# A state-space stage in which VectorE takes over one of two weighting products from POOL

## The reference, cut to what matters

```python
def step(h, inp):
    u_t, dt_t, B_t, C_t = inp
    dA = jnp.exp(-dt_t[..., None] * A)
    h = dA * h + (dt_t * u_t)[..., None] * B_t[:, None, :]
    y = jnp.einsum('bdn,bn->bd', h, C_t)
    return (h, y)
```

## Time and profile before

| what | us |
|---|---|
| median of three runs | 7111.84 |
| lowest and highest of them | 7104.78, 7119.30 |
| the profiled execution | 7122.96 |
| its span, first to last instruction | 7121.2 |

### The profile page before, as it was taken

One profiled execution on the slowest core, in us unless ns is written; L12 is line 12 of the kernel. 1 busy time (PEld: TensorE's weight loads), 2 busy tenths in 40 slices (PEclk: granted clock), 3 DMA queues, 4 the chain that ended last, 5 costly groups with the idle time before them and its releaser, 6 DMA issues. The chain is left out here.

```text
span 7121.2 us, 150074 instructions
## 1 busy us (share of the span) xinstructions
PE 5984.3 (84%) x47596; PEld 3842.3 (54%) x47596; DVE 5970.1 (84%) x12264; ACT 3439.2 (48%) x6820; POOL 2652.3 (37%) x1391
## 2 busy tenths in 40 slices
PE   5777888888888887988988988986888888888888
PEld 1224555555555554565565566565555555555555
DVE  5988888888888885998998998996979797979796
ACT  3335666666666662222222222222657575656565
POOL 1444444444444441122122122221535353535353
PEclk7998999999999998998998998988999999999999
DMA  0002222222222210000000000000212121212121
GB/s 14 0 0 63 59 52 59 52 59 52 59 52 59 53 46 13 1 1 1 1 1 1 1 1 1 1 0 16 60 50 61 51 60 51 63 49 62 50 63 37
DMA packets 159623, 244.44 MB, mean 34 GB/s; under 512 B 36596, under 2 KB 57008, under 8 KB 157494
## 3 DMA queue, kind: packets, MB, share of 16 engines
q1 hardware_dynamic: 159158, 238.71, 13.3%
HBM read 36.20 MB, written 1.05 MB: 5 GB/s over the span
## 5 line engine op out<-in xcount | busy, mean ns | idle before, releaser
L879 POOL TENSOR_TENSOR f_rope<-f_rope,f_t 128x1024 f32<-128x1024 f32 x384 | 918.5, 2392 | 1247.7 <-DVE f_t L775 1247.7
L1315 PE MATMUL psum<-tk_kT,tk_qs 128*128 128x512 f32 (+3 forms) x4128 | 1263.7, 467 | 9.1 <-POOL tk_qs L1548 9.1
L882 POOL TENSOR_TENSOR f_rope<-f_rope,f_rn 128x1024 f32<-128x1024 f32 x384 | 903.7, 2353 | 778.3 <-DVE f_rn L762 763.3
L1548 POOL TENSOR_TENSOR tk_qs<-tk_qT,tk_mix 128x1024 f32<-128x1024 f32 x258 | 499.2, 1938 | 1587.5 <-PE psum L1316 1423.2
L1315 PEld LDWEIGHTS psum<-tk_kT,tk_qs 128*128 128x128 f32 x4128 | 757.3, 208 | 440.5 <-issue 298.4
L775 DVE TENSOR_TENSOR f_t<-f_raw,f_rot 128x512 f32<-128x512 f32 x768 | 903.0, 1214 | 0.0
L454 PE MATMUL psum<-f_wqkv,f_xs 128*128 128x512 f32 x1536 | 785.0, 619 | 104.2 <-DMA f_wqkv<-in_Wqkv 56.1
L1505 DVE MAX8 tk_m<-tk_work 128x8 f32<-128x528 f32 (+3 forms) x1792 | 818.4, 497 | 2.0 <-DVE tk_work L1511 1.5
L1511 DVE MATCH_REPLACE8 tk_work<-tk_m,tk_work 128x400 f32<-128x400 f32 (+3 forms) x1536 | 745.3, 492 | 1.3 <-issue 1.0
L771 DVE TENSOR_TENSOR f_rope<-f_raw,f_rot 128x1024 f32<-128x1024 f32 x384 | 582.9, 1518 | 20.7 <-ACT f_raw L600 19.6
L600 ACT ACTIVATE f_raw<-psum 128x512 f32<-128x512 f32 x768 | 454.6, 595 | 249.2 <-PE psum L454 209.4
(11 more groups left out here) (234 smaller groups left out, 10764.0 us busy)
## 6 DMA issues: line engine op xcount, KB each, us to landing
f_v<-f_v_tok SPq DMA_DIRECT2D x1152, 128.0 KB, 2.4
f_v<-f_v_tok SPq DMA_DIRECT2D x768, 64.0 KB, 2.0
f_wqkv<-in_Wqkv SPq DMA_DIRECT2D x12, 1536.0 KB, 6.7
f_wo<-in_Wo SPq DMA_DIRECT2D x12, 512.0 KB, 4.1
f_w<-in_W SPq DMA_DIRECT2D x12, 341.0 KB
f_w<-in_W SPq DMA_DIRECT2D x24, 64.0 KB
tk_wkv<-in_Wkv SPq DMA_DIRECT2D x1, 1024.0 KB, 6.0
out<-y_tok SPq DMA_DIRECT2D x4, 256.0 KB, 2.5
```

Source lines behind the costliest of these rows:

```text
L879: pool.tensor_tensor(part, part, t2[:, half, :, :], ALU.add).then_inc(s["rope_added"], 1)
L882: pool.tensor_tensor(part, part, rn[:, H * half:H * (half + 1)].unsqueeze(2).to_broadcast([P, H, DH]), ALU.mult).then_inc(s["add_done"], 1)
L1315: pe.matmul(psum[:, j, 0:n], qs[:, j, c, :], kT[:, c, 0:n], start=(c == 0), stop=False, skip_group_check=True)
L1548: pool.tensor_tensor(qs[:, j, :, :], qT[:, :, P * t:P * (t + 1)], mix[:, :, heads(p, j)].to_broadcast([P, PAIRS, P]), ALU.mult).then_inc(s ...
```

## The change

In the state-space block POOL forms `hc` for channel 0 alone. For channel 1 VectorE forms it, reading C from its PSUM bank and not from the copy `c_sb`. VectorE's product of index n - 1 stands in its program between `dbu` and the scan of channel 1 of index n; the last one, of index 15, follows the last scan. The semaphore `hc_done` becomes two, `hc0_done` and `hc1_done`. TensorE waits in addition for `hc1_done` of n - 2 before it spreads B and C of n, since C's bank has VectorE as a reader too. ACT's copy of C now waits for channel 0's product of n - 2 alone, and channel 1's scan has no wait of its own for `hc` any more. The whole diff:

```diff
--- before.py
+++ after.py
@@ -895,7 +895,7 @@
     with ExitStack() as ctx:
         load = names(ctx, "mw", nc, "loaded", "turned", "copied", "done")
         s = names(ctx, "mb", nc, "zeroed", "xz_full", "xz_evac", "conv_in", "conv_step", "silu", "u_done", "xd_full", "xd_evac", "dt_full", "dt_in", "dt_abs",
-                  "dt_exp", "dt_ln", "dt_max", "dt_done", "sel", "bc_full", "b_used", "c_copied", "da_done", "dbu", "scanned", "hc_done",
+                  "dt_exp", "dt_ln", "dt_max", "dt_done", "sel", "bc_full", "b_used", "c_copied", "da_done", "dbu", "scanned", "hc0_done", "hc1_done",
                   "y_full", "y_evac", "y_step", "yg_done", "out_full", "out_done", "staged", "copied", "scrap")
 
         def sb(name, shape, dt=F32):
@@ -1064,7 +1064,7 @@
                 with pe.Fori(0, B) as b:
                     def sums(n):
                         for c in range(CI):
-                            pe.wait_ge(s["hc_done"], 1 + CI * DS * b + CI * n + c + 1)
+                            pe.wait_ge(s[f"hc{c}_done"], 1 + DS * b + n + 1)
                             if n == 0 and c == 0:
                                 pe.wait_ge(s["y_evac"], 1 + CI * b)
                             pe.matmul(psum[:, 4 + c, :], k.ident[:, :], hc[:, (CI * n + c) % 4, :], start=(n == 0), stop=(n == DS - 1),
@@ -1074,9 +1074,11 @@
                         if n >= 2:
                             pe.wait_ge(s["b_used"], 1 + CI * (DS * b + n - 1))
                             pe.wait_ge(s["c_copied"], 1 + DS * b + n - 1)
+                            pe.wait_ge(s["hc1_done"], 1 + DS * b + n - 1)
                         else:
                             pe.wait_ge(s["b_used"], 1 + CI * DS * b)
                             pe.wait_ge(s["c_copied"], 1 + DS * b)
+                            pe.wait_ge(s["hc1_done"], 1 + DS * b)
                         for which in range(2):
                             pe.matmul(psum[:, 2 * which + n % 2, :], sel[:, DS * which + n, :], batch3(xd, b, P), start=True, stop=True).then_inc(s["bc_full"], 1)
                         if n >= 2:
@@ -1099,9 +1101,9 @@
                             act.activation(da[:, (CI * n + c) % 4, :], batch(dt, c, b), ACT.Exp, scale=neg_a[:, c, n:n + 1]).then_inc(s["da_done"], 1)
                         act.wait_ge(s["bc_full"], 1 + 2 * (DS * b + n) + 2)
                         if n >= 2:
-                            act.wait_ge(s["hc_done"], 1 + m0 - 2)
+                            act.wait_ge(s["hc0_done"], 1 + DS * b + n - 1)
                         else:
-                            act.wait_ge(s["hc_done"], 1 + CI * DS * b)
+                            act.wait_ge(s["hc0_done"], 1 + DS * b)
                         act.activation(c_sb[:, n % 2, :], psum[:, 2 + n % 2, :], ACT.Copy).then_inc(s["c_copied"], 1)
 
             @block.vector
@@ -1110,17 +1112,32 @@
                     for c in range(CI):
                         dve.tensor_tensor(dtu[:, c, :], batch(dt, c, b), batch(u, c, b), ALU.mult).then_inc(s["staged"], 1)
                     dve.wait_ge(s["staged"], 1 + CI * b + CI)
+
+                    def weighted(n):
+                        i = CI * n + 1
+                        m = CI * DS * b + i
+                        dve.wait_ge(s["scanned"], 1 + m + 1)
+                        dve.wait_ge(s["c_copied"], 1 + DS * b + n + 1)
+                        if i >= 4:
+                            dve.wait_ge(s["y_full"], 1 + m - 3)
+                        else:
+                            dve.wait_ge(s["y_full"], 1 + CI * DS * b)
+                        dve.tensor_tensor(hc[:, i % 4, :], hs[:, i % 4, :], psum[:, 2 + n % 2, :], ALU.mult).then_inc(s["hc1_done"], 1)
+
                     for n in range(DS):
                         for c in range(CI):
                             i = CI * n + c
                             m = CI * DS * b + i
                             dve.wait_ge(s["bc_full"], 1 + 2 * (DS * b + n) + 1)
                             dve.tensor_tensor(dbu[:, i % 4, :], dtu[:, c, :], psum[:, n % 2, :], ALU.mult).then_inc(s["b_used"], 1)
+                            if c == 1 and n:
+                                weighted(n - 1)
                             dve.wait_ge(s["b_used"], 1 + m + 1)
                             dve.wait_ge(s["da_done"], 1 + m + 1)
-                            if i >= 4:
-                                dve.wait_ge(s["hc_done"], 1 + m - 3)
+                            if c == 0 and n >= 2:
+                                dve.wait_ge(s["hc0_done"], 1 + DS * b + n - 1)
                             dve.tensor_tensor_scan(hs[:, i % 4, :], da[:, i % 4, :], dbu[:, i % 4, :], 0.0, ALU.mult, ALU.add).then_inc(s["scanned"], 1)
+                    weighted(DS - 1)
                     for c in range(CI):
                         dve.wait_ge(s["y_full"], 1 + CI * DS * b + CI * (DS - 1) + c + 1)
                         dve.scalar_tensor_tensor(tmp[:, c, :], batch(u, c, b), skip[:, c:c + 1], psum[:, 4 + c, :], ALU.mult, ALU.add).then_inc(s["y_evac"], 1)
@@ -1137,16 +1154,15 @@
             def _(pool):
                 with pool.Fori(0, B) as b:
                     for n in range(DS):
-                        for c in range(CI):
-                            i = CI * n + c
-                            m = CI * DS * b + i
-                            pool.wait_ge(s["scanned"], 1 + m + 1)
-                            pool.wait_ge(s["c_copied"], 1 + DS * b + n + 1)
-                            if i >= 4:
-                                pool.wait_ge(s["y_full"], 1 + m - 3)
-                            else:
-                                pool.wait_ge(s["y_full"], 1 + CI * DS * b)
-                            pool.tensor_tensor(hc[:, i % 4, :], hs[:, i % 4, :], c_sb[:, n % 2, :], ALU.mult).then_inc(s["hc_done"], 1)
+                        i = CI * n
+                        m = CI * DS * b + i
+                        pool.wait_ge(s["scanned"], 1 + m + 1)
+                        pool.wait_ge(s["c_copied"], 1 + DS * b + n + 1)
+                        if i >= 4:
+                            pool.wait_ge(s["y_full"], 1 + m - 3)
+                        else:
+                            pool.wait_ge(s["y_full"], 1 + CI * DS * b)
+                        pool.tensor_tensor(hc[:, i % 4, :], hs[:, i % 4, :], c_sb[:, n % 2, :], ALU.mult).then_inc(s["hc0_done"], 1)
 
 
 def tokens(x, b):
```

## The result

The changed kernel takes 7135.8 us (median of 7 runs, 7131.6 to 7150.9), the kernel before 7113.6 (7 runs, 7104.8 to 7119.3): ratio 1.0036, 95% interval 1.0025 to 1.0048. It is **slower by some 22 to 26 us**, where 38 us less were forecast and the range ended at 7095. The profiled execution of the changed kernel is one of its fastest, 7131.7 (span 7129.5); that of before, 7123.0 (span 7121.2), is slower than all seven of its runs, so the two profiles show only 8.3 of the difference.

The account below looks back on a forecast made before the run. VectorE was taken to set the state-space loop's pace, its scans blocked by POOL's products. Per batch 8.9 plus 0.25 plus 0.4 is 9.5, 38 us in four batches, off the median 7111.84: 7074 us, range 7057 to 7095.

Parts of the forecast that it names:

- the sum: State-space stage: per batch 15 x 0.59 = 8.9, plus 0.25, plus 0.4, is 9.5; four batches 38 us.
- the five rivals: Alternatives: blocked product 3%, scans long regardless 3%, longer TensorE loop 17%, TensorE at 1.2 GHz 1%, nothing left 4%.
- the prediction's last sentence: Forecast is wrong if the stage saves under 25 us, or if time appears in later stages.
- (a): VectorE in the state-space loop: gains 16 products per batch, 0.65 us each, starting 0.60 apart, unblocked by POOL.
- (b): POOL loses every second product: channel 0's scan takes 1.23, channel 1's ends 1.08 after POOL's; one n 4.41, not 5.00.
- Rivals 1 and 2: State-space loop: POOL blocks the new product, 13 us lost (3%); or scans stay long whatever POOL does, 7150 us (3%).
- (c): TensorE's new wait before B's broadcast: hidden with 0.03 us to spare, the loop by this way 4.38 us.
- rival 3: Loop through TensorE longer than its tie: one n 4.6 to 4.8, gain 12 to 24 us less; chance 17%.
- (e): Batch ends: first n unchanged at 4.7 us; `tmp` starts some 0.85 after the last scan, gain 0.25; clock gain 0.4.
- The 0.4 us per batch from the clock: Batch end: denser TensorE work may run output products partly at 2.4 GHz; 0 to 1.8 per batch, 0.4 taken.
- Rival 4: State-space loop: TensorE falls to 1.2 GHz, 8 passes take 6.9 us per n, 114 us lost, 7226; chance 1%.

Follow-up runs that it names:

- after_bfirst: Changed kernel plus 30 TensorE filler increments, TensorE's wait for VectorE's product moved from ahead of B's spread to ahead of C's; 7068.7 us, ratio 0.9944.
- before_dve48: Kernel before plus 48 VectorE increments of an unused semaphore ahead of the state-space loop; 7093.2 us, ratio 0.9972.
- before_mid241: Kernel before plus 241 TensorE increments of an unused semaphore in the set-up of the top-k attention; 7202.3 us, ratio 1.0125.

## Why the prediction was wrong

**The step that failed** is one sentence behind the sum: "Stages behind this one start after a barrier and have the same code." They have the same code, at another place. Fifteen fewer TensorE instructions put the second stack's loop where it is fetched anew at each of its twelve returns, which makes that stage 54.7 us longer in the profile. It is shown by taking it away (15 fillers, in two places), by bringing it into the kernel before (241, in two places) and by moving it to the first stack (180). Why this place and not the old one stays open. None of the five rivals had it, though the prediction's last sentence names the sign, time that appears in later stages. The loss outweighs all that the stage gave.

Point by point, within the stage:

- (a), (b) held: the new product 0.68, channel 0's scan 1.22, channel 1's end 1.08 behind POOL's, one n 4.41 as forecast. Rivals 1 and 2 are refuted by these rows. But the 5.00 to which I compared it was one of two orders; the other, 4.30, would have left the change nothing to gain. It stood in no row of before that I could read.
- (c) held in the steady part, and rival 3 with it failed there: the loop through TensorE ends at 4.40, forecast 4.38. It was mis-sized at a batch's start. I looked at the first n and said no change; the second and third take 5.35 to 5.56 and 4.7 to 5.0. The timeline of the second batch shows why:

```profile
244.97 0.68 DVE L1125 TENSOR_TENSOR mb_hc<-mb_hs,psum 128x512 f32<-128x512 f32 x1
...
245.79 3.75 PE L1083 MATMUL psum<-mb_xd,mb_sel 128*128 x4 [5.82 <-DVE mb_hc L1125]
...
247.88 0.69 DVE L1132 TENSOR_TENSOR mb_dbu<-mb_dtu,psum 128x512 f32<-128x512 f32 x1 [0.84 <-PE psum L1083]
```

TensorE had nothing to do for 5.82 us until the first new product, comes back at half clock (granted 0.50 from 245.7 to 249.3 us, three passes in 2.90) and lets VectorE wait 0.84 for B. Moving that wait (after_bfirst) took the second n's loss away and left the third's. Per batch the two cost some 1.4 us, 6 in all.

- (e) was right in size on the last scan. It ends at 226.30 and `tmp` starts 0.79 later, forecast 0.85 (1.09 before):

```profile
224.82 1.48 DVE L1139 TENSOR_TENSOR_SCAN mb_hs<-mb_da,mb_dbu 128x512 f32<-128x512 f32 x1
...
226.49 0.69 DVE L1125 TENSOR_TENSOR mb_hc<-mb_hs,psum 128x512 f32<-128x512 f32 x1 [0.19 <-DVE mb_hs L1139]
...
227.09 0.74 DVE L1143 SCALAR_TENSOR_TENSOR mb_tmp<-mb_u,mb_skip,psum 128x512 f32<-128x512 f32 x1
```

The 0.4 us per batch from the clock didn't come: VectorE waited 15.4 us for the output products, 15.0 before.
- Rival 4 didn't come: TensorE's clock over the loop is 0.92, as before.

- Sum: 38 us forecast for the stage, 30.5 between first and last scan and 32.3 up to the next stage's load. The missing 6 are about what the two slow n cost. The 1.6 from the clock are missing too; the first batch's first n, 3.68 instead of 4.69, gives 1.0 of them back. With TensorE's place put right the whole kernel gains about 57 by its medians, 46 by its profile; the part above 32 lies in stages not touched. Some 10 of it may be VectorE's place in the second stack (before_dve48); the rest isn't explained.

## What to carry to other kernels

A change in one stage moves the instructions of every stage behind it. Where a long loop returns many times (1620 instructions here), compare the packets of the instruction queues and the "issue" idle time at the loop's first line before judging the change, and try it with a handful of filler instructions. When two engines block each other, look for a second order in which they could lock, since the one seen may not be the cheap one; one wait can choose it.

## What the runs showed that was not expected

- Semaphore increments follow each other on TensorE every 0.15 us (241 of them in 36.9 us in before_mid241).
- POOL's product and VectorE's scan have two steady orders, 5.00 and 4.30 us per state index with the same instructions; which one a batch falls into is set by whether POOL's first product comes up before or with the second scan's beginning, 0.12 to 0.27 us apart here.
- In the fast case the loop of 1620 instructions ran its second and third iterations, 138 us, without a single packet on q8; in the slow one each of them fetched 9. The Trainium skill's section named above also says that the instruction memory is only 2 cache lines. The fast case doesn't agree for TensorE: a body of over six blocks is kept there.
